# Opening of an attention kernel: layout and order of the first loads, and the order of the first products

## The chip, the cores and the metric

The kernel runs on one core of a Trainium2 chip. The metric is the device time of one execution in microseconds (us): 339.38 is the median of three runs (339.26 to 340.31). The profile is of one further execution, whose own time was 339.0 us; its span from first to last instruction is 337.2 us.

A core has a matmul engine (TensorE, PE in the rows, with its weight loads as PEld), three elementwise engines (VectorE or DVE, ScalarE or ACT, GpSimd or POOL), and a queue of instructions (SyncE, SP) which here issues all transfers between HBM and the on-chip memory SBUF. Matmul results appear in eight banks of another memory, PSUM. Each engine takes its instructions in order; semaphores order the engines against each other.

## What is computed

One layer with causal attention and a linear feed-forward part, both followed by a layer norm, for 1024 tokens of width 512, in float32. Cut to what matters:

```python
q = (x @ Wq) -> 32 heads of 16;  k, v = (x @ Wkv) -> 8 groups of 16 each (4 heads share a group)
scores = q @ k.T, causal; weights = softmax(scores / 4); ctx = weights @ v
x = layernorm(x + ctx @ Wo + bo)
x = layernorm(x + x @ W.T + bias + lora(x))
```

## The kernel before

**Precision by parts.** A float32 operand of a product is split into a high half (the value rounded to a type that TensorE takes at full speed, made by ScalarE) and a low half (the remainder, made by VectorE, later by GpSimd). A product of two operands is three matmuls: high by high, high by low, low by high. So one projection of 128 output columns for 512 tokens, over an inner dimension of 4 chunks of 128, is 12 matmuls of 512 columns. K and Q results are then split into three bf16 parts: ScalarE copies the first (L732), VectorE makes the rest (L958), ScalarE the middle part (L737), VectorE (in the opening, L968) or GpSimd (L582) the low part.

**Units.** Work is done in 16 units, one for each half of the tokens (queries) and each group of 4 heads. For every unit the maxima of the scores are found first, from score matmuls (L1135, called chunks; `chunk_scores` on TensorE, `chunk_max` on VectorE, L917 and L910), then the scores are computed again with the maximum subtracted as additional rows of the operand (L1359), the exponential is taken (ScalarE, L856) and multiplied with V (L1337). The rows come from small bf16 operands QS (queries) and KS (keys) with the parts of a head stacked on the partitions. For all units but the first, the parts are stored to HBM (L479) and loaded back in that arrangement (`load_keys` L490, `load_queries` L502); for the first unit they are moved within the chip by matmuls with selecting matrices: `direct_keys` (3 matmuls) and `direct_queries` (12), L1149, whose results ScalarE (L750, L755) and VectorE (L1070) copy to KS and QS. I call these the move of K and the moves of Q.

**The opening.** `PLAN_A` names the first eight jobs in TensorE's order and how many chunks must have been issued when each ends: K, Q part 0, V, Q part 1, the turning of V, Q part 2, then K and V of the second half of the tokens. Each job is cut in three parts, and chunks stand between parts. The first chunk stands behind the first third of Q part 1; it waits until all four moved queries and the moved keys have been copied. The moves of Q stand behind the second third of V, the move of K between Q part 0 and V.

The transfers are issued in this order by the queue: K's weights wk (L467), the four chunks of the turned x, first half of the tokens (L465, `load_turned(0)`), the part of Wq for Q part 0 (L470), V's weights wv (L471), the rest of Wq (L472), and x's second half (L465). Each is its own semaphore; all are 256 KB but the rest of Wq, 768 KB. A row of x's chunk is a run of 2 KB in HBM; wk, wv and the first part of Wq come in four runs of 512 B for each partition, the rest of Wq in runs of 1.5 KB.

ScalarE's list starts: high half of wk (L818), of x's chunks 0 to 3 (L815), of the first part of Wq (L803), the first part of K's result (L732), high half of wv (L824), middle part of K, high half of Wq's part 1, first part of Q, copy of the moved keys, middle part of Q, high halves of Wq's parts 2 and 3, two copies of moved queries. VectorE's (L1046 and on) starts with the low halves in the same order (L1048, L1043, L1053), then the rest of K (L958), the low half of wv (L962), the low part of K (L968), and the same two for Q. GpSimd makes constants and selecting matrices until 13 us, then the low halves of Wq's parts 1 to 3 (L599) and of x's second half (L606). TensorE begins with nine idle matmuls (`run_idle`, L1288); products are L1195, in `halves`, called by `pe_job`.

K takes its products chunk by chunk of x as the halves come; Q part 0 waits for its weights and has all of its products behind K's.

## Time and profile before

| | |
|---|---|
| median of three runs | 339.38 us (339.26 to 340.31) |
| the profiled execution | 339.0 us, of which the span is 337.2 |
| TensorE busy | 322.3 us, 96% of the span |
| VectorE, ScalarE, GpSimd busy | 256.6, 216.5, 135.3 us |
| mean granted TensorE clock | 0.996 of full speed |
| chain that ended last, by engine | PE 71%, DMA 7%, DVE 7%, ACT 4%, issue 4%, queue 3%, POOL 2% |

Matmuls are pipelined: one of 512 columns lasts 0.4 us or more in the rows while the next starts 0.2 us after it, so starts are to be compared, and the starts of weight loads (PEld) show them best. A row that merges several instructions gives the start of the first, the time from there to the end of the last, and their number. In brackets is how long the engine had been idle and what released it.

### The profile page before, as it was taken

How to read it: one execution, taken by the hardware profiler on the slowest of the kernel's cores; microseconds unless marked ns; L12 is line 12 of the kernel's file. 1: busy time of each engine (PE TensorE's matmuls, PEld its weight loads, DVE VectorE, ACT ScalarE, POOL GpSimd, SP SyncE). 2: the span in 40 equal slices, each digit the busy share in tenths (PEclk: the TensorE clock that was granted, in tenths of full speed). 3: DMA queues.
4: the chain of work that ended last, by engine and by line, in shares of the span. 5: the costliest groups of instructions: out<-in, count | busy, mean ns of one | idle time of the engine just before them, and what ended most of it. 6: DMA issues, size and time to landing. Idle time of an engine off the chain costs nothing.

```text
span 337.2 us, 7240 instructions
## 1 busy us (share of the span) xinstructions
PE 322.3 (96%) x2487; PEld 169.7 (50%) x2487; DVE 256.6 (76%) x787; ACT 216.5 (64%) x418; POOL 135.3 (40%) x268
## 2 busy tenths in 40 slices
PE   8999989999999999999999999999999999999992
PEld 3676445455353344454444544544544434558882
DVE  3557968978888899888889889888886961047664
ACT  4754737645657796848757668478585786952431
POOL 8845325433547585347222123212141122331553
PEclk9999999999999999999999999999999999999998
DMA  6886494874244120020010100000000000000002
GB/s 202 289 163 170 132 183 120 225 230 118 53 148 155 36 63 5 3 47 3 3 48 33 48 4 3 0 31 3 3 0 3 32 2 1 2 33 1 0 33 93
DMA packets 16643, 22.96 MB, mean 68 GB/s; under 512 B 3232, under 2 KB 10560, under 8 KB 16608
## 3 DMA queue, kind: packets, MB, share of 16 engines
q1 hardware_dynamic: 16608, 22.51, 24.4%
q8 instruction: 20, 0.33, 0.4%
q14 instruction: 15, 0.12, 0.1%
HBM read 16.29 MB, written 6.03 MB: 66 GB/s over the span
## 4 chain that ended last, share of the span: by engine, by line
PE 71%; DMA 7%; DVE 7%; ACT 4%; issue 4%; SPq 3%; POOL 2%; POOLq 0%; DVEq 0%; ACTq 0%
PE PS L1337 18%; PE PS L1195 16%; PE PS L1135 15%; PE PS L1359 15%; DMA QS<-NMR 3%; ACT PB L856 2%; PE PS L1263 2%; PE PS L1255 2%; DVE scrap L917 2%; DVE MX L910 2%; DMA scr_q<-parts 2%; DMA X<-in_L_attn_x_turned_dram 1%; SPq L490 1%; PE PS L1149 1%; SPq L502 1%
## 5 line engine op out<-in xcount | busy, mean ns | idle before, releaser
L856 ACT ACTIVATE PB<-PS 128x512 f32<-128x512 f32 x288 | 155.6, 604 | 59.1 <-PE PS L1359 57.9
L917 DVE CUSTOM_DVE_ANT_0 scrap<-PS,mask 128x128 bf16<-128x128 f32 (+3 forms) x256 | 111.5, 487 | 17.6 <-PE PS L1135 17.1
L1135 PE MATMUL PS<-KS,QS 96*128 96x512 bf16 (+3 forms) x384 | 107.9, 329 | 2.1 <-DVE MX L910 1.0
L1359 PE MATMUL PS<-QS,KS 99*128 99x512 bf16 x288 | 106.2, 381 | 1.8 <-DMA QS<-NMR 1.4
L910 DVE TENSOR_REDUCE MX<-PS 128x1 f32<-128x512 f32 x128 | 81.9, 684 | 12.4 <-PE PS L1135 11.7
L696 POOL TENSOR_SCALAR_AFFINE_SELECT PB<-PB 128x256 f32<-128x256 f32 (+1 forms) x96 | 46.4, 485 | 104.3 <-ACT PB L856 101.2
L1337 PE MATMUL PS<-PB,VX 128*32 128x256 f32 (+1 forms) x1280 | 78.8, 364 | 0.6 <-ACT PB L856 0.3
L1135 PEld LDWEIGHTS PS<-KS,QS 96*128 96x128 bf16 x384 | 32.9, 98 | 49.4 <-issue 13.6
L1337 PEld LDWEIGHTS PS<-PB,VX 128*32 128x32 f32 x1280 | 33.5, 109 | 41.9 <-issue 19.0
L1195 PE MATMUL PS<-XT,WQ 128*128 128x512 f32 x144 | 45.4, 439 | 0.5 <-ACT NMR L744 0.4
L1359 PEld LDWEIGHTS PS<-QS,KS 99*128 99x128 bf16 x288 | 27.5, 98 | 31.4 <-ACT PB L856 7.9
L1195 PEld LDWEIGHTS PS<-XT,WQ 128*128 128x128 f32 x144 | 26.6, 193 | 9.5 <-DVE XT L1043 1.5
L1195 PE MATMUL PS<-XT 128*128 128x512 f32 x96 | 28.1, 426 | 0.6 <-DVE MX L910 0.6
L1195 PE MATMUL PS<-WQ,XT 128*128 128x512 f32 x96 | 28.3, 427 | 0.0
L677 POOL TENSOR_SCALAR mv<-mv 128x1 f32<-128x1 f32 x15 | 3.4, 228 | 48.7 <-DVE mv L1012 48.6
L917 DVE DVE_READ_ACCUMULATOR2_ANT MX<- 128x1 f32 x256 | 21.2, 83 | 0.0
L1195 PEld LDWEIGHTS PS<-XT 128*128 128x128 f32 x96 | 17.9, 189 | 4.6 <-DVE MX L910 1.1
L1195 PEld LDWEIGHTS PS<-WQ,XT 128*128 128x128 f32 x96 | 17.9, 189 | 4.1
L770 ACT ACTIVATE RAW<-PS 128x256 f32<-128x256 f32 x32 | 12.4, 387 | 11.2 <-PE PS L1337 11.0
L788 ACT ACTIVATE TC<-RAW,shift,rstd 128x512 f32<-128x512 f32 x7 | 5.7, 817 | 13.4 <-POOL shift L679 13.4
L732 ACT ACTIVATE parts<-PS 128x512 bf16<-128x512 f32 x10 | 6.0, 597 | 10.7 <-PE PS L1195 10.7
L658 POOL CAST NMPS<-NM 128x16 bf16<-128x16 f32 x15 | 3.3, 221 | 21.7 <-DVE NM L931 21.7
(93 smaller groups left out, 263.6 us busy)
## 6 DMA issues: line engine op xcount, KB each, us to landing
scr_q<-parts SPq DMA_DIRECT2D x8, 384.0 KB, 4.0
QS<-scr_q SPq DMA_DIRECT2D x15, 192.0 KB, 2.9
X<-in_L_attn_x_turned_dram SPq DMA_DIRECT2D x8, 256.0 KB, 6.3
X<-in_L_attn_x_dram SPq DMA_DIRECT2D x8, 256.0 KB, 3.1
out_dram<-TC SPq DMA_DIRECT2D x8, 256.0 KB, 2.0
QS<-scr_q SPq DMA_DIRECT2D x15, 128.0 KB, 3.0
RAW<-in_L_attn_Wo_dram SPq DMA_DIRECT2D x2, 512.0 KB, 5.9
RAW<-in_L_ffn_W_dram SPq DMA_DIRECT2D x2, 512.0 KB, 9.0
```

What stands on the lines that cost most here:

```text
L696: nc.gpsimd.affine_select(out=blk, in_=blk, compare_op=ALU.is_ge, fill=0.0, base=0, pattern=[[0, len(heads)], [1, P]], channel_multiplier=-1)\
L732: nc.scalar.activation(parts[:, m % 2, 0, :], job_bank(n), ACT.Copy).then_inc(act_copied, 1)
L770: nc.scalar.activation(RAW[:, u, cols], PS[:, PV_BANK, cols], ACT.Copy).then_inc(raw_out, 1)
L856: nc.scalar.activation(PB[:, cyc % NP_BUF, k, :], PS[:, score_bank(e), :], ACT.Exp, scale=SCALE)\
L910: nc.vector.tensor_reduce(part[:, j0:j1, 0:1], bank, AX, ALU.max).then_inc(max_read, 1)
L917: last = nc.vector.tensor_tensor_reduce(out=scrap[:, n % 2, (j - j0) * width:(j - j0 + 1) * width], in0=bank[:, j - j0, :], in1=mask[:, HT ...
L1135: last = nc.tensor.matmul(PS[:, CHUNK_BANK[n], k * width:(k + 1) * width], QS[0:ROWS, u % SLOTS, j, qb * P:(qb + 1) * P], KS[0:ROWS, g, k0 ...
L1195: last = nc.tensor.matmul(bank, lhs(a, c), rhs(b, c), start=(k == 0), stop=(k == len(terms) - 1))
L1255: last = nc.tensor.transpose(bank[:, g * P:(g + 1) * P], RAW[:, h * G + g0 + g, qb * P:(qb + 1) * P], ident[:, :])
L1263: last = nc.tensor.transpose(bank[:, c * P:(c + 1) * P], src[:, c * P:(c + 1) * P], ident[:, :])
L1337: last = nc.tensor.matmul(PS[32 * j:32 * j + 32, PV_BANK, s * HQ + skip:(s + 1) * HQ], VX[:, key_blocks(cyc)[i], u % G, :], PB[:, cyc % NP ...
L1359: nc.tensor.matmul(PS[:, score_bank(e), :], KS[0:NROW, u % G, kb * P:(kb + 1) * P], QS[0:NROW, u % SLOTS, heads[0]:heads[-1] + 1, s * HQ + ...
```

## The change

1. The host lays Wq and Wkv out so that each partition's piece of a load is one run: wk, wv and Wq's first part 2 KB, the rest of Wq 3 times 2 KB in one piece. Amounts are unchanged.
2. The loads go in the order wk, x's chunks 0 and 1, Wq's first part, x's chunks 2 and 3, wv, the rest of Wq, x's second half. ScalarE and VectorE split in that order, wv too (ahead of K's result).
3. TensorE's first 24 products (`first_products`) go K0, K1, Q0, Q1, K2, Q2, K3, Q3 (the digit is x's chunk), three each. V's twelve follow whole, taking those with the low half of wv last; then the move of K and the moves of Q.
4. ScalarE copies K's and Q's first parts one behind the other, then the middle parts of both, then splits Wq's part 1 and copies the moved keys. VectorE makes both rests, then both low parts.

```diff
@@ -22,9 +22,10 @@
     HD = 16
     H = D // HD
-    G = wkv.shape[2] // HD
+    G = wkv.shape[2] // (D // P) // HD
     REP = H // G
     NC = D // P
     NT = T // P
@@ -337,7 +338,7 @@
         X1B = [TC[:, 4, :], TC[:, 5, :]]
         OUT = [TC[:, 6, :], TC[:, 7, :]]
         a_raw, bT = TC[:, 0, :], TC[:, 8, :]
-        wk_raw, wv_raw = (TC[:, n, :].rearrange("p (c n) -> p c n", c=NC) for n in (2, 3))
+        wk_raw, wv_raw = TC[:, 2, :], TC[:, 3, :]
         bo_bc = TC[:, 4, :]
         vT = TC[:, 5, :]
         rest = TC[:, 6:8, :]
@@ -444,11 +445,14 @@
 
             return x_low[h], c + 1
 
+        def by_chunk(raw):
+            return raw.rearrange("p (c n) -> p c n", c=NC)
+
         def wq_part(half, k):
             return WQ[:, half, :, k * P:(k + 1) * P]
 
         def wq_part_raw(k):
-            return wq_raw[:, :, k * P:(k + 1) * P]
+            return wq_raw[:, k, :].rearrange("p (c n) -> p c n", c=NC)
 
         x_v = x.rearrange("a (h b p) d -> (a h) p b d", h=2, p=P)
         out_v = out.rearrange("a (b p) d -> (a b) p d", p=P)
@@ -458,18 +462,18 @@
 
         @block.sync
         def _(sp):
-            def load_turned(h):
+            def load_turned(h, chunks=range(NC)):
 
                 half = slice(h * HT, (h + 1) * HT)
-                for c in range(NC):
+                for c in chunks:
                     sp.dma_start(XR[:, c, half], xt[c * P:(c + 1) * P, half]).then_inc(x_in[h][c], 16)
 
-            sp.dma_start(wk_raw, wkv[0].rearrange("(c p) n -> p c n", p=P)).then_inc(wk_in, 16)
-            load_turned(0)
-            wq_v = wq.rearrange("(c p) n -> p c n", p=P)
-            sp.dma_start(wq_raw[:, :, 0:P], wq_v[:, :, 0:P]).then_inc(wq_in, 16)
-            sp.dma_start(wv_raw, wkv[1].rearrange("(c p) n -> p c n", p=P)).then_inc(wv_in, 16)
-            sp.dma_start(wq_raw[:, :, P:D], wq_v[:, :, P:D]).then_inc(wq_rest_in, 16)
+            sp.dma_start(wk_raw, wkv[0]).then_inc(wk_in, 16)
+            load_turned(0, range(0, 2))
+            sp.dma_start(wq_raw[:, 0, :], wq[:, 0, :]).then_inc(wq_in, 16)
+            load_turned(0, range(2, NC))
+            sp.dma_start(wv_raw, wkv[1]).then_inc(wv_in, 16)
+            sp.dma_start(wq_raw[:, 1:NC, :], wq[:, 1:NC, :]).then_inc(wq_rest_in, 16)
 
             def parts_to_dram(n):
 
@@ -815,18 +819,20 @@
                 nc.scalar.activation(XT[:, 0, c, half], XR[:, c, half], ACT.Copy).then_inc(x_high, 1)
 
             act.wait_ge(wk_in, 16)
-            nc.scalar.activation(WQ[:, 0, :, D:D + KD], wk_raw, ACT.Copy).then_inc(wk_high, 1)
-            for c in range(NC):
-                x_high_half(0, c)
+            nc.scalar.activation(WQ[:, 0, :, D:D + KD], by_chunk(wk_raw), ACT.Copy).then_inc(wk_high, 1)
+            x_high_half(0, 0)
+            x_high_half(0, 1)
             wq_high_half(0)
+            x_high_half(0, 2)
+            x_high_half(0, 3)
+            act.wait_ge(wv_in, 16)
+            nc.scalar.activation(WQ[:, 0, :, D + KD:D + 2 * KD], by_chunk(wv_raw), ACT.Copy).then_inc(wv_high, 1)
             act_job(JOB["K", 0, 0])
-            act.wait_ge(wv_in, 16)
-            nc.scalar.activation(WQ[:, 0, :, D + KD:D + 2 * KD], wv_raw, ACT.Copy).then_inc(wv_high, 1)
+            act_job(JOB["Q", 0, 0])
             middle_part(0)
+            middle_part(1)
             wq_high_half(1)
-            act_job(JOB["Q", 0, 0])
             direct_keys()
-            middle_part(1)
             wq_high_half(2)
             wq_high_half(3)
             for j in (0, 2):
@@ -957,16 +963,6 @@
                     s = m % 2
                     nc.vector.tensor_tensor(rest[:, s, :], bank, parts[:, s, 0, :], ALU.subtract)\
                         .then_inc(job_freed, 1)
-                    if m == 0:
-                        dve.wait_ge(wv_high, 1)
-                        nc.vector.tensor_tensor(WQ[:, 1, :, D + KD:D + 2 * KD], wv_raw,
-                                                WQ[:, 0, :, D + KD:D + 2 * KD].bitcast(F32), ALU.subtract)\
-                            .then_inc(wv_split, 1)
-                    if m < 2:
-                        dve.wait_ge(rest_split, m + 1)
-                        dve.wait_ge(*freed(JOBS[n]))
-                        nc.vector.tensor_tensor(parts[:, s, 2, :], rest[:, s, :], parts[:, s, 1, :], ALU.subtract)\
-                            .then_inc(parts_ready, 1)
                 else:
                     nc.vector.tensor_tensor(w_raw[:, c, :], bank, w_raw[:, c, :], ALU.add).then_inc(job_freed, 1)
 
@@ -1045,15 +1041,27 @@
 
             nc.vector.memset(Z[:, :], 0.0).then_inc(zeros, 1)
             dve.wait_ge(wk_high, 1)
-            nc.vector.tensor_tensor(WQ[:, 1, :, D:D + KD], wk_raw, WQ[:, 0, :, D:D + KD].bitcast(F32), ALU.subtract)\
+            nc.vector.tensor_tensor(WQ[:, 1, :, D:D + KD], by_chunk(wk_raw), WQ[:, 0, :, D:D + KD].bitcast(F32), ALU.subtract)\
                 .then_inc(wk_split, 1)
-            for c in range(NC):
-                x_low_half(0, c)
+            x_low_half(0, 0)
+            x_low_half(0, 1)
             dve.wait_ge(wq_high, 1)
             nc.vector.tensor_tensor(wq_part(1, 0), wq_part_raw(0), wq_part(0, 0).bitcast(F32), ALU.subtract)\
                 .then_inc(wq_split, 1)
+            x_low_half(0, 2)
+            x_low_half(0, 3)
+            dve.wait_ge(wv_high, 1)
+            nc.vector.tensor_tensor(WQ[:, 1, :, D + KD:D + 2 * KD], by_chunk(wv_raw),
+                                    WQ[:, 0, :, D + KD:D + 2 * KD].bitcast(F32), ALU.subtract).then_inc(wv_split, 1)
+            dve_job(JOB["K", 0, 0])
+            dve_job(JOB["Q", 0, 0])
+            for m in range(2):
+                dve.wait_ge(rest_split, m + 1)
+                dve.wait_ge(*freed(PROJ[m]))
+                nc.vector.tensor_tensor(parts[:, m, 2, :], rest[:, m, :], parts[:, m, 1, :], ALU.subtract)\
+                    .then_inc(parts_ready, 1)
             dve.wait_ge(consts, 3)
-            for n in range(NJOB_A):
+            for n in range(2, NJOB_A):
                 for part in range(3):
                     if part == 2:
                         dve_job(n)
@@ -1195,6 +1203,21 @@
                     last = nc.tensor.matmul(bank, lhs(a, c), rhs(b, c), start=(k == 0), stop=(k == len(terms) - 1))
                 return last
 
+
+            def first_products():
+
+                pe.wait_ge(wk_high, 1)
+                for kind, c in (("K", 0), ("K", 1), ("Q", 0), ("Q", 1), ("K", 2), ("Q", 2), ("K", 3), ("Q", 3)):
+                    n, col, high, low = {"K": (0, D, wk_high, wk_split), "Q": (1, 0, wq_high, wq_split)}[kind]
+                    for k, (a, b) in enumerate(((0, 0), (1, 0), (0, 1))):
+                        pe.wait_ge(*((high, 1), (low, 1), x_split(0, c))[k])
+                        if k == 0:
+                            pe.wait_ge(x_high, c + 1)
+                        last = nc.tensor.matmul(job_bank(n), WQ[:, a, c, col:col + P], XT[:, b, c, 0:HT],
+                                                start=(c == k == 0), stop=(c == NC - 1 and k == 2))
+                    if c == NC - 1:
+                        last.then_inc(job_done, 1)
+
             def pe_job(n, part, parts=3):
 
                 kind, h, c = JOBS[n]
@@ -1208,25 +1231,18 @@
                 if kind in ("K", "V", "Q"):
                     if part == 0:
 
-                        if (kind, h) not in (("K", 0), ("Q", 0)) or c:
+                        if (kind, h) != ("V", 0):
                             pe.wait_ge(*{"K": (wk_split, 1), "V": (wv_split, 1), "Q": (wq_split, c + 1)}[kind])
                         if kind != "K":
                             for cc in range(NC):
                                 pe.wait_ge(*x_split(h, cc))
-
                     terms, ready = TERMS, {}
-                    if (kind, h) == ("K", 0):
-                        terms = [(cc, a, b) for cc in range(NC) for a, b in ((0, 0), (1, 0), (0, 1))]
-                        for cc in range(NC):
-                            ready[cc, 0, 0] = [(x_high, cc + 1)] + ([(wk_high, 1)] if cc == 0 else [])
-                            ready[cc, 1, 0] = [(wk_split, 1)] if cc == 0 else []
-                            ready[cc, 0, 1] = [x_split(0, cc)]
                     if (kind, h) == ("K", 1):
                         for cc in range(NC):
                             ready[cc, 0, 0] = [x_split(1, cc)]
-                    if (kind, h, c) == ("Q", 0, 0):
+                    if (kind, h) == ("V", 0):
                         terms = [(cc, 0, b) for cc in range(NC) for b in (0, 1)] + [(cc, 1, 0) for cc in range(NC)]
-                        ready = {(0, 0, 0): [(wq_high, 1)], (0, 1, 0): [(wq_split, 1)]}
+                        ready = {(0, 0, 0): [(wv_high, 1)], (0, 1, 0): [(wv_split, 1)]}
                     col = {"K": D, "V": D + KD, "Q": c * P}[kind]
                     last = halves(bank, lambda a, cc: WQ[:, a, cc, col:col + P],
                                   lambda a, cc: XT[:, a, cc, half], part, parts, terms, ready)
@@ -1290,17 +1306,17 @@
             pe.wait_ge(zeros, 1)
             run_idle(9)
             pe.wait_ge(consts, 1)
-            for n in range(NJOB_A):
+            first_products()
+            for n in range(2, NJOB_A):
                 for part in range(3):
                     pe_job(n, part)
                     for k in chunks_of_job(n, part):
                         chunk_scores(k)
-                    if JOBS[n] == ("V", 0, 0) and part == 1:
+                    if JOBS[n] == ("V", 0, 0) and part == 2:
+                        direct_keys()
                         direct_queries()
                     if JOBS[n] == ("V", 1, 0) and part == 1:
                         direct_rows()
-                if JOBS[n] == ("Q", 0, 0):
-                    direct_keys()
             pe.wait_ge(consts, 6)
             FIRST_BEHIND = {3 + n % RING: JOBS[n] for n in range(NJOB_A - RING, NJOB_A)}
 
@@ -1421,8 +1437,10 @@
     wkv = wkv.reshape(d, -1, 2, hd)
     laid = dict(inputs)
     laid["L0_attn_x_turned"] = x[0].T
-    laid["L0_attn_Wq"] = wq.reshape(d, nc, 128 // hd, hd).transpose(0, 1, 3, 2).reshape(d, d)
-    laid["L0_attn_Wkv"] = _np.stack([wkv[:, :, 0].transpose(0, 2, 1).reshape(d, -1), wkv[:, :, 1].reshape(d, -1)])
+    wq = wq.reshape(nc, 128, nc, 128 // hd, hd).transpose(1, 2, 0, 4, 3)
+    laid["L0_attn_Wq"] = wq.reshape(128, nc, d)
+    wkv = _np.stack([wkv[:, :, 0].transpose(0, 2, 1).reshape(d, -1), wkv[:, :, 1].reshape(d, -1)])
+    laid["L0_attn_Wkv"] = wkv.reshape(2, nc, 128, -1).transpose(0, 2, 1, 3).reshape(2, 128, -1)
     laid["L0_ffn_lora_B"] = _np.asarray(inputs["L0_ffn_lora_B"]).transpose(0, 2, 1).reshape(128, d)
     laid["L0_ffn_W"] = _np.asarray(inputs["L0_ffn_W"]).T
     laid["L0_ffn_lora_weights"] = _np.repeat(_np.asarray(inputs["L0_ffn_lora_weights"]), 16).reshape(128, 1)
```

## Rows read from the trace of the kernel before

**Rows 1.** Stretches: length, busy us (count) of PE, PEld, DVE, ACT, POOL, clock, DMA

```profile
33.40:50.00 16.60, 14.61 (x103) 7.41 (x103) 14.53 (x65) 9.27 (x17) 4.96 (x11) 1.00 0.76 156
...
100.00:150.00 50.00, 49.31 (x425) 22.27 (x425) 44.83 (x132) 38.10 (x79) 31.15 (x50) 1.00 0.19 52
```

**Rows 2.** Timeline of TensorE: start, us, line, tiles, count [idle <-releaser]

```profile
1.24 4.02 PE L1288 MATMUL PS<-Z 128*128 128x512 bf16 x9 [1.24 <-DVE Z L1046]
...
5.68 0.29 PEld L1195 LDWEIGHTS PS<-XT,WQ 128*128 128x128 f32 x1 [0.25 <-DVE XT L1043]
...
7.02 0.19 PEld L1195 LDWEIGHTS PS<-XT,WQ 128*128 128x128 f32 x1 [0.31 <-DVE XT L1043]
...
9.61 2.82 PEld L1195 LDWEIGHTS PS<-XT,WQ 128*128 128x128 f32 x13 [0.43 <-DVE XT L1043]
...
12.98 0.38 PEld L1149 LDWEIGHTS PS<-parts,PB 128*96 128x96 bf16 x3 [0.55 <-DVE parts L968]
...
13.45 1.79 PEld L1195 LDWEIGHTS PS<-XT,WQ 128*128 128x128 f32 x8
...
15.76 2.32 PEld L1149 LDWEIGHTS PS<-parts,PB 128*96 128x96 bf16 x12 [0.51 <-DVE parts L968]
...
18.17 1.79 PEld L1195 LDWEIGHTS PS<-XT,WQ 128*128 128x128 f32 x8
...
20.24 0.23 PEld L1135 LDWEIGHTS PS<-KS,QS 96*128 96x128 bf16 x4 [0.27 <-issue]
```

**Rows 3.** Timeline of ScalarE: splits and copies of the opening

```profile
3.51 0.63 ACT L818 ACTIVATE WQ<-TC 128x512 fp32r<-128x512 f32 x1 [1.44 <-DMA TC<-in_L_attn_Wkv_dram]
...
4.23 0.63 ACT L815 ACTIVATE XT<-X 128x512 fp32r<-128x512 f32 x1
...
5.61 0.63 ACT L815 ACTIVATE XT<-X 128x512 fp32r<-128x512 f32 x1 [0.75 <-DMA X<-in_L_attn_x_turned_dram]
...
8.20 0.63 ACT L815 ACTIVATE XT<-X 128x512 fp32r<-128x512 f32 x1 [0.60 <-DMA X<-in_L_attn_x_turned_dram]
...
9.01 0.63 ACT L803 ACTIVATE WQ<-RAW 128x512 fp32r<-128x512 f32 x1 [0.18 <-DMA RAW<-in_L_attn_Wq_dram]
...
10.14 0.60 ACT L732 ACTIVATE parts<-PS 128x512 bf16<-128x512 f32 x1 [0.50 <-PE PS L1195]
...
12.89 0.60 ACT L732 ACTIVATE parts<-PS 128x512 bf16<-128x512 f32 x1 [0.16 <-PE PS L1195]
...
14.88 1.14 ACT L803 ACTIVATE WQ<-RAW 128x512 fp32r<-128x512 f32 x2
```

**Rows 4.** Timeline of the queue: the issue of Wq's first part

```profile
3.25 0.43 SPq L470 DMA_DIRECT2D RAW<-in_L_attn_Wq_dram  x1
```

**Rows 5.** Stretches with their DMA share and GB/s at the end

```profile
3.00:7.20 4.20, 4.20 (x12) 1.92 (x10) 2.12 (x3) 2.12 (x4) 3.96 (x13) 1.00 0.87 253
7.50:8.70 1.20, 1.02 (x4) 0.48 (x3) 0.74 (x1) 0.60 (x2) 1.14 (x4) 1.00 1.06 314
...
11.00:13.00 2.00, 1.87 (x10) 1.21 (x8) 1.83 (x3) 1.53 (x4) 1.94 (x2) 1.00 1.05 386
```

**Rows 6.** Timeline of VectorE: last copy of moved queries

```profile
18.59 0.69 DVE L1070 CAST QS<-PS 96x512 bf16<-96x512 f32 x1 [0.61 <-PE PS L1149]
```

**Rows 7.** Timeline of GpSimd: low half of Wq's part 1

```profile
13.21 1.30 POOL L599 TENSOR_TENSOR WQ<-RAW,WQ 128x512 fp32r<-128x512 f32 x1
```

**Rows 8.** Chain of waits, in order of time, and ScalarE's copy of the rows

```profile
26.09 2.56 DMA scr_q<-parts
...
45.21 4.76 DMA QS<-NMR
...
43.29 0.27 ACT L744 ACTIVATE NMR<-PS 48x128 bf16<-48x128 f32 x1
```

**Rows 9.** Timelines: six key loads issued, first chunk of unit 1

```profile
19.60 2.79 SPq L490 DMA_DIRECT2D KS<-scr_k  x6
...
31.36 0.40 PE L1135 MATMUL PS<-KS,QS 96*128 96x128 bf16 x4
```

## The prediction

> **What bounds the kernel now.** I began with the table of stretches. From 50 us on TensorE has no room: in the stretch 100 to 150 it is busy 49.31 of 50 us [rows 1], and nothing there is tied to the clock on the wall, only to the work before it. So whatever the opening is shorter by should arrive at the end, if the stretch from 20 to 50 us passes it on. The change touches the first 20 us alone, so the quantity to forecast is one moment: the first score matmul of the maxima, "chunk 0", which starts at 20.24 [rows 2]. The weight loads on TensorE's queue show what stands before it. The last product of K's first half waits 0.43 us for VectorE and starts at 9.61; it and Q's twelve run 0.22 us apart ((2.82 - 0.19)/12). The move of K waits until 12.98, eight V products follow 0.23 apart, the moves of Q wait 0.51 us until 15.76, take 2.41 us (to 18.17), then four V and four Q products, then chunk 0 [rows 2]. That is 44 matmuls in 10.63 us; at 0.22 they need 9.7, so 0.9 us of it is waiting. Before 9.61 TensorE is starved: 12 products in the time that the loads of x leave it.
>
> The loads show themselves on ScalarE, which splits each as it lands: wk 3.51, x's chunk 0 4.23, chunk 1 5.61, chunk 3 8.20 (1.32 a step on average), wq's part 9.01 [rows 3]. The queue has issued them all much earlier, by 3.68 [rows 4], so the 16 DMA engines set the pace, not the issues.
>
> **What the change removes, adds and moves.** No matmul, copy or byte goes. TensorE has the same 55 matmuls before chunk 0: 24 products of K and Q, 12 of V, 3 + 12 moves, 4 of the next Q. Nine of Q's products (chunks 0 to 2) move ahead of K's last one, into idle time; V's twelve come together, ahead of both moves; and wq's part is loaded third of five, not last.
>
> *When wq's part is split.* It is now behind x's chunk 1, as x's chunk 2 was. Its 256 KB in runs of 2 KB are a load such as trace of before has in this stretch only for x: step 1.32, so ScalarE starts it at 5.61 + 1.32 = 6.93. The bounds: at the 314 GB/s of the stretch in which wq's part and V's weights went in runs of 512 B, 262 KB take 0.83 us, so 6.44; at the 386 GB/s of later 2 KB loads 0.68, so 6.29 [rows 5]. On the slow side, x's first step was 1.38 and the last two 1.30 each on average; one of 1.6, 0.2 beyond the longest, makes 7.2. I take 6.9, because the nearest row has both the size of run and the stretch. The first load, wk, gets the same runs; I leave it where it is, with 0.2 us either way (its 262 KB at 314 and at 386 GB/s differ by 0.15; at 253 it would be 0.2 longer than at 314). x's chunks 2 and 3 go back by one step, to 8.3 and 9.6.
>
> The Trainium skill, "DMA: Bandwidth & Descriptors", Specifications, gives 512 B as the least transfer at full rate; by that the longer runs gain nothing at all. The trace agrees only in part: full-rate stretches show 314 GB/s with mostly 512 B and 386 with 2 KB, yet the cold loads of x, already in 2 KB, reach 253 [rows 5]. By the rule the run length is worth 0, by the two faster rows 0.15 us a load; the sum has 0.
>
> *To K's last product.* From ScalarE's start on a chunk to the weight load that waited for its low half 1.41 us pass (8.20 to 9.61) [rows 2, 3]. TensorE takes its stream in order, so Q's second product starts at 6.9 + 1.41 = 8.3, and all behind it is ready in time or nearly so: thirteen steps of 0.22 later, at 11.17, comes K's last product. (x's chunk 3 alone would allow 9.6 + 1.41 = 11.0.) So K is finished 1.5 us later than now, Q's last product starts at 11.8; it is 12.24 now (9.61 + 2.82 - 0.19).
>
> *To the moves.* K's last product and Q's three: 0.88. V's twelve at 0.22 to 0.23: 2.7. K's three moves: 0.6 (now 0.47 from 12.98 to 13.45, with weight loads running ahead). Q's moves could start at 11.17 + 4.15 = 15.3. Do they find their data? From the start of ScalarE's copy of Q to the moves 12.89 to 15.76, 2.87, go by now, and K's chain took 10.14 to 12.98, 2.84 [rows 2, 3]. Q's copy can start 0.53 after its last weight load, as K's does now (9.61 to 10.14), at 12.3, so the parts are there at 15.2: just in time. VectorE has both rests back to back, then both low parts, and V's low half (one more half such as x's, now between them) falls before K's rest. V's weights are split on ScalarE ahead of K's copy, a wait that is new in this place: K's copy, Q's copy and both middle parts stand behind it. It costs nothing as long as V's weights land by about 10.9; one more load of 1.32 after 9.6 is 10.9. That cover is thin: each 0.1 us beyond it goes on the path.
>
> *To chunk 0.* 2.41 for Q's moves, four products at 0.23 and the 0.27 of the issue wait [rows 2]: 3.6, so 18.9. VectorE's last copy ends 18.59 + 0.69 - 15.76 = 3.52 after the moves' start [rows 6], at 18.8. ScalarE now has the two last splits of wq (1.14 [rows 3]) between its copy of K's move and its two of Q's; from K's last move at 15.1 that is 0.53, 0.6, 1.14 and 1.2 more: 18.5. Both fit, with little to spare. GpSimd's low half of wq's part 1 takes 1.30 [rows 7], from about 15.1, and is used at 17.7. Chunk 0 at 18.9 for 20.24: **1.4 us** earlier.
>
> *Passed on?* From 20 to 50 the path runs through the queue: the store of Q's second part at 26.09, key and query loads, at 45.21 the maxima's move, which lands at 49.97 where TensorE waits for it; the rows for that move are ready on ScalarE at 43.56 [rows 8]. That both arms start from work behind chunk 0 says that both come 1.4 us earlier. What doesn't come 1.4 earlier are the keys of the other units, whose loads follow the landing of Q's first parts: those are ready 0.5 earlier, not 1.4. The six loads are issued from 19.60, over by 22.39, and are wanted at 31.36 [rows 9]; even 5 us to landing (the last move of the maxima took 4.76) leaves 4 us, then 3. So all of 1.4 passes. Against the profiled execution (span 337.2, time 339.0) this is 337.6; against the median 339.38, which lies 0.4 above it, 338.0. I forecast 338.0.
>
> **Rivals.**
> - *The runs pay.* Wq's part is split at 6.3 to 6.5 and wk lands 0.15 sooner; the whole stream behind Q's second product moves with it one to one, to a gain of 1.8 to 2.2: about 337.4. For it: the rates of 314 and 386. Against: 253 in the very stretch.
> - *Loads later than taken.* Five cold 2 KB loads, each as x's, and wk too; the in-order stream waits at Q's first product with K's behind it. Every 0.1 us costs 0.1: at 7.3 the gain is 1.0, at 8.3 none. Likewise V's weights landing after 10.9, held before K's copy. About 338.8.
> - *Absorbed.* Chunk 0 comes as forecast, but one link between 20 and 50 does not: VectorE is busy 14.53 of 16.60 us there [rows 1]. About 339.2. Against: its work also hangs on chunk 0.
> - *Slower: TensorE's clock.* The granted column reads 1.00, yet idle matmuls of 512 columns take 4.02 us for nine, 0.43 apart with the tail of the last, the 1.2 GHz level, and 0.22 is that of 2.4; K's weight loads fall from 0.29 to 0.19 us between 5.68 and 7.02 [rows 2], so that is where the level rises. In the changed kernel TensorE has one product between 7.2 and 8.3 us, while it waits for wq. If it stays or falls back to 1.2 GHz there, a product costs 0.21 more: seven of them eat the gain, twelve make it slower by more than 0.3%, and the 18 products from there to V's make 3.8 - 1.4 = 2.4 slower, 341.8. Against it: waits of 0.25 and 0.31 us between products now did not keep the level from rising, and one of 0.43 did not bring it down.
>
> The Trainium skill, "TensorE: Matmul & The Clock Gate", Part 1, says that the array's default is the half rate, that activity releases it and idleness brings it back. The rise in the trace agrees; no row of before shows a fall in the opening.
>
> **How the numbers follow.** Forecast 0.48 (gain 1.05 to 1.8: 337.6 to 338.3); runs pay 0.15; loads later 0.15; absorbed 0.15; clock 0.07. What a measurement here can tell from no change is about 0.3%, 1.0 us. Faster: 0.48 + 0.15 = 0.63. Within: 0.15 + 0.15 = 0.30. Slower 0.07. The range goes from 337.0 (a gain of 2.4) to 339.5 (nothing left, and the scatter of the runs), which leaves out the slower case and little else.
>
> **What would show it.** In the changed kernel's rows: ScalarE's split of wq near 6.9 and x's last near 9.6; one unbroken run of products from 8.3 with K's last at 11.2 and Q's 0.66 behind; no idle before K's move; Q's moves from 15.3; chunk 0 at 18.9; the maxima's move landing at 48.6. If wq is split at 6.4 or before, the step of 1.32 was wrong; if weight loads take 0.29 after 8.3, the clock rival holds; if chunk 0 is early and 49.97 hasn't moved, it is absorbed. A gap before Q's moves says that the chain of parts, with V's split before it, was late.

## The result: slower by 0.7%, and the profile after

The changed kernel takes 341.63 us (median of 22 executions, 339.26 to 344.27), the kernel before 339.83 in the same runs (338.34 to 340.43). The ratio is 1.0067, with a 95% interval of 1.0048 to 1.0085: slower by 1.6 to 2.9 us, where 1.4 us faster had been forecast. The profiled execution took 340.97 us with a span of 339.3, 2.1 us more than that of before. Comparisons here leave out executions that are more than 1.5% above the fastest of their kernel.

ScalarE's timeline of the changed kernel shows what came when; it answers to [rows 3]. L819 are x's chunks, L807 Wq's parts, L829 V's weights, L736 the first parts of K and Q.

```profile
3.51 0.63 ACT L822 ACTIVATE WQ<-TC 128x512 fp32r<-128x512 f32 x1 [1.44 <-DMA TC<-in_L_attn_Wkv_dram]
4.12 0.63 ACT L819 ACTIVATE XT<-X 128x512 fp32r<-128x512 f32 x1
5.41 0.63 ACT L819 ACTIVATE XT<-X 128x512 fp32r<-128x512 f32 x1 [0.65 <-DMA X<-in_L_attn_x_turned_dram]
8.32 0.63 ACT L807 ACTIVATE WQ<-RAW 128x512 fp32r<-128x512 f32 x1 [2.28 <-DMA RAW<-in_L_attn_Wq_dram]
9.77 1.28 ACT L819 ACTIVATE XT<-X 128x512 fp32r<-128x512 f32 x2 [0.82 <-DMA X<-in_L_attn_x_turned_dram]
11.08 0.63 ACT L829 ACTIVATE WQ<-TC 128x512 fp32r<-128x512 f32 x1
14.84 1.29 ACT L736 ACTIVATE parts<-PS 128x512 bf16<-128x512 f32 x2 [3.13 <-PE PS L1216]
```

K's weights and x's chunks 0 and 1 are there as forecast or sooner. Wq's first part is 2.9 us behind chunk 1, not 1.3: the engine stood idle for 2.28 us. The loads issued behind it are late too. ScalarE waits 0.82 us more for x's chunk 2 and starts it at 9.77, where 8.3 was forecast, so here it could have split nothing in the meantime. From the issue of Wq's load to its landing:

```profile
DMA to landing us min/median/max: 6.1/6.1/6.1
```

TensorE's weight loads, which answer to [rows 2] (the last row is chunk 0):

```profile
6.98 0.19 PEld L1216 LDWEIGHTS PS<-XT,WQ 128*128 128x128 f32 x1 [0.53 <-DVE XT L1039]
9.00 0.19 PEld L1216 LDWEIGHTS PS<-XT,WQ 128*128 128x128 f32 x1 [1.83 <-ACT WQ L807]
9.73 5.34 PEld L1216 LDWEIGHTS PS<-XT,WQ 128*128 128x128 f32 x17 [0.54 <-DVE WQ L1049]
15.11 2.69 PEld L1203 LDWEIGHTS PS<-XT,WQ 128*128 128x128 f32 x12
17.84 3.15 PEld L1157 LDWEIGHTS PS<-parts,PB 128*96 128x96 bf16 x15
...
22.30 0.24 PEld L1143 LDWEIGHTS PS<-KS,QS 96*128 96x128 bf16 x4 [0.35 <-issue]
```

Between the last product of chunk 1 (6.98) and Q's second product (9.73) there is one product. Then 17 products take 5.34 us, 0.32 each, where [rows 2] has 0.22. The moves start without a wait (17.84). The stretches say why the products are slow; the columns are the stretch, its length, busy us (count) of TensorE, the granted clock as a share of 2.4 GHz, and the DMA engines' busy share and GB/s:

```profile
5.00:7.00 2.00, 1.76 (x6) 1.00 0.91 207
7.00:9.00 2.00, 0.48 (x1) 1.00 0.89 284
9.00:11.00 2.00, 1.78 (x7) 1.00 1.02 410
11.00:13.00 2.00, 2.00 (x6) 0.51 0.98 384
13.00:15.00 2.00, 2.00 (x7) 0.64 0.34 131
15.00:17.00 2.00, 2.00 (x11) 1.00 0.00 1
```

In 7 to 9 us TensorE is busy 0.48 of 2 us; from 11 on the granted clock is at its lower level (1.2 GHz) for about 3.4 us ((1 - 0.51) x 2 / 0.5 and (1 - 0.64) x 2 / 0.5), then back at 2.4. Chunk 0 starts at 22.30 and not 20.24. The chain of waits leads from Wq's load to the first transfer of the maxima's rows:

```profile
2.17 6.13 DMA RAW<-in_L_attn_Wq_dram
...
9.73 5.77 PE PS L1216 x17
...
47.48 4.79 DMA QS<-NMR
```

It lands at 52.27; from [rows 8] it was 49.97. So 2.1 us at chunk 0 became 2.3 at 52 us and 2.1 at the end.

Three explanations were to be told apart: **A**, TensorE's clock falls because it idles; **B**, runs of 2 KB are slow this early; **C**, the load's place in the order. Later B was split into **D/F**, the distance between the runs, **G**, the spread over untouched memory, and **E**, the run length as such.

### The profile page after: what moved, and what is told of

Its sections match the earlier page's. It is cut to its first block, busy times and chain, and to the rows that moved or that the text cites. A ratio compares the mean times of both kernels' runs of the same rounds, so it can differ in the third digit from the quotient of the medians.

```text
span 339.3 us, 7246 instructions
## 1 busy us (share of the span) xinstructions
PE 322.7 (95%) x2487; PEld 170.9 (50%) x2487; DVE 256.6 (76%) x787; ACT 216.3 (64%) x418; POOL 134.4 (40%) x268
## 4 chain that ended last, share of the span: by engine, by line
PE 72%; DMA 8%; DVE 6%; issue 4%; ACT 4%; SPq 3%; POOL 2%; POOLq 0%; DVEq 0%; ACTq 0%
PE PS L1353 18%; PE PS L1203 16%; PE PS L1143 15%; PE PS L1375 15%; DMA QS<-NMR 3%; ACT PB L862 2%; PE PS L1279 2%; PE PS L1271 2%; DMA scr_q<-parts 2%; DVE scrap L923 2%; DVE MX L916 2%; DMA RAW<-in_L_attn_Wq_dram 2%; PE PS L1216 2%; SPq L494 1%; SPq L506 1%
## 5 line engine op out<-in xcount | busy, mean ns | idle before, releaser
L1203 PE MATMUL PS<-XT,WQ 128*128 128x512 f32 x120 | 37.5, 435 | 0.4 <-ACT NMR L748 0.4
L1203 PEld LDWEIGHTS PS<-XT,WQ 128*128 128x128 f32 x120 | 22.0, 190 | 5.9 <-ACT NMR L748 1.3
L736 ACT ACTIVATE parts<-PS 128x512 bf16<-128x512 f32 x10 | 6.0, 597 | 13.4 <-PE PS L1203 10.2
```

Source lines behind the costliest of these rows:

```text
L1203: last = nc.tensor.matmul(bank, lhs(a, c), rhs(b, c), start=(k == 0), stop=(k == len(terms) - 1))
```

## Experiments

Each kernel is compared with the kernel before on the same chip. The experiments ran on four chips (e1 to e4, e5 to e8, e9 to e12, e13 to e15), so kernels of different groups are compared only through the kernel before. The ratio is not the quotient of the two medians beside it. Where the two differ much (e7, e10, e11, e13), the size of the effect is the less certain.

"Landing" is issue to landing of Wq's first part in the one profiled execution. It is comparable between the kernels of this table, which load that part third (behind x's chunk 1). One trace each is thin: the same loads landed in 4.6 and 5.5 us (e2 and e4), and, two places later in the order, in 5.5 and 6.4 (e11 and e15).

| kernel | runs of Wq's first part | landing, us | median, before's | ratio, 95% |
|---|---|---|---|---|
| changed | 2 KB, 8 KB apart | 6.1 | 341.63, 339.83 | 1.0067 (1.0048 to 1.0085) |
| e13 changed, again | the same | 6.4 | 341.28, 339.95 | 1.001 (0.9968 to 1.0051) |
| e3 idle matmuls | the same | 6.7 | 341.51, 340.14 | 1.0025 (0.9999 to 1.0051) |
| e10 | 2 KB, 16 KB apart | 4.3 | 341.56, 339.67 | 1.0023 (0.999 to 1.0056) |
| e9 | 2 KB, 10 KB apart | 4.4 | 339.06, 339.67 | 0.9976 (0.9951 to 1.0002) |
| e5 | 2 KB, one piece | 4.3 | 338.34, 339.97 | 0.9956 (0.9928 to 0.9984) |
| e14 | 2 KB, one piece | 4.8 | 338.36, 339.95 | 0.9945 (0.9917 to 0.9974) |
| e6, x too | 2 KB, one piece | 4.8 | 338.96, 339.97 | 0.9971 (0.9947 to 0.9994) |
| e2 | 512 B, 2 KB apart | 4.6 | 339.18, 340.14 | 0.9967 (0.9939 to 0.9994) |
| e4, e2 with idle matmuls | 512 B, 2 KB apart | 5.5 | 341.03, 340.14 | 1.002 (0.9995 to 1.0045) |
| e7 | 512 B, 2 KB apart | 4.3 | 338.87, 339.97 | 0.9989 (0.996 to 1.0018) |

### The layout or the order: e1 and e2

e1 is the kernel before with change 1 alone; e2 is the changed kernel without it. Of e2's edit against the changed kernel, the line that loads Wq's first part:

```diff
-            sp.dma_start(wq_raw[:, 0, :], wq[:, 0, :]).then_inc(wq_in, 16)
+            sp.dma_start(wq_raw[:, :, 0:P], wq_v[:, :, 0:P]).then_inc(wq_in, 16)
```

> The kernel before with the new layout alone: wk, wv and Wq's first part in runs of 2 KB, order of loads and of products as before. Theory A (the clock fall made the change slow, the runs are neutral): within 0.5 us of before, Wq's part split near 9.0. Theory B (2 KB runs from HBM are slow to land this early): Wq's part is split at 9.8 or later and x's chunks shift too, 0.7 to 1.5 us slower than before. Theory C (the place of Wq's load in the order made it late): as A, no difference.

> The changed kernel with the old layout: runs of 512 B, but the new order of loads and products. Theory A: the clock still falls when TensorE waits for Wq, so still 1 to 2 us slower than before. Theory B: Wq's part is split at 6.5 to 6.9 and not at 8.3, the stream runs from 8.0, TensorE hardly waits, the clock stays, and the kernel is 1 to 2 us faster than before. Theory C: Wq's part still at 8 or later, as slow as the changed kernel.

e1: 0.9985 (0.996 to 1.001), no difference. But its ScalarE timeline shows the slow load even there, 2.05 us behind x's chunk 3, where [rows 3] has 0.81:

```profile
7.81 0.63 ACT L817 ACTIVATE XT<-X 128x512 fp32r<-128x512 f32 x1 [0.45 <-DMA X<-in_L_attn_x_turned_dram]
9.86 0.63 ACT L805 ACTIVATE WQ<-RAW 128x512 fp32r<-128x512 f32 x1 [1.41 <-DMA RAW<-in_L_attn_Wq_dram]
```

K's chain doesn't wait for it, and the executions show no loss, though in this trace chunk 0 came at 20.89, 0.65 us later than before. e2: 0.9967 (0.9939 to 0.9994), 1.1 us faster. The new layout costs nothing measurable in the old order, the new order gains with the old layout, and only both together lose: C falls. TensorE's weight loads of e2 are the forecast nearly to the letter, Q's second product at 8.37 (8.3), chunk 0 at 19.32 (18.9), the clock at 1.00:

```profile
8.37 3.73 PEld L1217 LDWEIGHTS PS<-XT,WQ 128*128 128x128 f32 x17 [0.40 <-DVE WQ L1050]
...
14.86 3.15 PEld L1158 LDWEIGHTS PS<-parts,PB 128*96 128x96 bf16 x15
...
19.32 0.24 PEld L1144 LDWEIGHTS PS<-KS,QS 96*128 96x128 bf16 x4 [0.35 <-issue]
```

### The clock: e3, e4, e15

All three have ten idle matmuls where TensorE waits for Wq: e3 is the changed kernel with them, e4 is e2 with them, e15 is described below.

```diff
+                        if (kind, c) == ("Q", 0) and k < 2:
+                            run_idle((8, 2)[k])
```

> The changed kernel with ten more idle matmuls: eight before the first product of Q, two before its second, where TensorE waits for Wq's part. Nothing else differs. Theory A: the granted clock stays at 1.00, eight products at 0.43 become 0.22, so about 1.7 us faster than the changed kernel, close to before (0 to +0.5 us). Theory B or C alone (the late load is all of the loss): no change against the changed kernel, +2 us against before.

> Old layout, new order, with the ten idle matmuls. If the runs of 2 KB make the load late (B) and the clock is the other half (A), this is the fastest of the four, 1 to 1.5 us faster than before, a little behind the kernel without idle matmuls where the clock stays anyway. If the place in the order makes the load late (C), it is like the kernel with idle matmuls and the new layout, level with before.

e3 gets 1.0025 where the changed kernel had 1.0067; the changed kernel's second measurement (e13, 1.001) can't be told from it, so the executions alone don't show that filling helps here. The trace does: the load is as late (6.7), and the 17 products take 3.75 us, at a granted clock of 1.00, for 5.34, and chunk 0 comes at 21.30 for 22.30:

```profile
9.00:11.00 2.00, 1.39 (x6) 1.00 1.03 418
11.00:13.00 2.00, 2.00 (x11) 1.00 1.02 398
```

```profile
9.61 0.19 PEld L1218 LDWEIGHTS PS<-XT,WQ 128*128 128x128 f32 x1 [1.17 <-ACT WQ L807]
...
10.33 3.75 PEld L1218 LDWEIGHTS PS<-XT,WQ 128*128 128x128 f32 x17 [0.27 <-DVE WQ L1049]
```

e4 missed what I expected of an early load: 1.002 (0.9995 to 1.0045), slower than e2. The idle matmuls are themselves in the way. In its trace (of an execution of 344.79 us, 3.8 above its median, with x's chunk 1 late as well) the last product of x's chunk 1 starts at 8.52, the idle ones run until 10.3, and the high half of Wq had been ready since 8.5. Filling is a trade, not a gift.

### Lateness by order alone: e11 and e15

e11 has the fast layout (e5's), but issues Wq's part behind x's chunks 2 and 3, while the engines still take it third. e15 adds the ten idle matmuls to that. Of e11's edit, against e5:

```diff
-            load_turned(0, range(0, 2))
+            load_turned(0)
             sp.dma_start(wq_raw[:, 0, :], wq[0]).then_inc(wq_in, 16)
-            load_turned(0, range(2, NC))
```

> Wq in one piece per part (the fast layout), but its first part issued behind x's chunks 2 and 3, while ScalarE, VectorE and TensorE still take it in third place. It makes Wq late by order alone: split at 7.8 to 8.5, as late as in the changed kernel. If lateness in that place is the whole mechanism (TensorE stands with Q's first product, and the clock may fall), it gives back most of the gain of the early one: 1 to 2 us slower than the same layout with Wq third, +0 to +1 us against before. If the layout costs in another way than by this wait, it stays 1 us or more faster than before.

> The kernel with Wq in one piece but issued too late (behind x's chunks 2 and 3, +1.8 us against before), with eight idle matmuls ahead of Q's first product and two ahead of its second, so that the wait is as long but TensorE isn't idle in it. If the fall of TensorE's clock is a cost of its own beside the wait, the eight or so products at half rate (0.43 for 0.22 each) go: granted clock 1.00 from 5 to 20 us, 1 to 1.7 us faster than without them, +0.1 to +0.8 us against before. If the wait is all, no change: +1.8 us.

e11: 1.0053 (1.0026 to 1.0079), 1.8 us slower than before, 3.3 slower than the same layout in time (e5, through before), and beyond the 0 to 1 us that I expected. The split is at 8.60, x's chunks 2 and 3 had landed and stood behind it in ScalarE's list, and the clock falls as in the changed kernel:

```profile
5.66 0.63 ACT L818 ACTIVATE XT<-X 128x512 fp32r<-128x512 f32 x1 [0.75 <-DMA X<-in_L_attn_x_turned_dram]
8.60 0.63 ACT L806 ACTIVATE WQ<-RAW 128x512 fp32r<-128x512 f32 x1 [2.31 <-DMA RAW<-in_L_attn_Wq_dram]
```

```profile
7.00:9.00 2.00, 0.64 (x2) 1.00 1.04 395
9.00:11.00 2.00, 1.71 (x3) 0.55 1.06 408
11.00:13.00 2.00, 2.00 (x7) 0.60 0.92 339
13.00:15.00 2.00, 2.00 (x11) 1.00 0.04 14
```

e15: 0.9985 (0.9956 to 1.0014), no difference from before. The loss is gone, but so is the gain: a late load with TensorE kept busy about cancels the forecast 1.4. From e15 to e11 it is 2.3 us by the ratios, whose intervals do not meet, and that is what the idle matmuls save: 3.4 us at half the clock are 1.7 of it. I had expected 1 to 1.7. e15's one trace shows the clock at 1.00 from 5 to 23 us but not the time: it is of an execution of 343.58 us, 3.3 above its median, in which x's chunk 0 was split at 5.70 and Wq's part at 9.51, and chunk 0 of the maxima came at 22.88.

```profile
22.88 0.24 PEld L1142 LDWEIGHTS PS<-KS,QS 96*128 96x128 bf16 x4 [0.35 <-issue]
```

### What makes the load late: e5, e6, e7, e9, e10, e14

e5 stores Wq part by part, so that each part is one piece of 256 KB; e6 does the same with x's chunks; e7 puts only Wq back to 512 B; e9 and e10 pad Wq's rows to 10 and 16 KB; e14 takes the first part out into one piece, and leaves the rest in runs of 6 KB, as the changed kernel has them, but now directly behind one another. Of e5's edit:

```diff
-            sp.dma_start(wq_raw[:, 0, :], wq[:, 0, :]).then_inc(wq_in, 16)
+            sp.dma_start(wq_raw[:, 0, :], wq[0]).then_inc(wq_in, 16)
...
-    wq = wq.reshape(nc, 128, nc, 128 // hd, hd).transpose(1, 2, 0, 4, 3)
-    laid["L0_attn_Wq"] = wq.reshape(128, nc, d)
+    wq = wq.reshape(nc, 128, nc, 128 // hd, hd).transpose(2, 1, 0, 4, 3)
+    laid["L0_attn_Wq"] = wq.reshape(nc, 128, d)
```

> The changed kernel with Wq laid out part by part: runs of 2 KB as in the changed kernel, but those of the first part lie directly behind one another (256 KB in one piece), not 8 KB apart. Theory D (it is the distance of the runs, 8 KB, that makes Wq's load slow): Wq's part is split one step of 0.8 to 1.3 us behind x's chunk 1, near 6.5, the clock stays, 2.5 to 3.5 us faster than the changed kernel, so 0.5 to 1.2 faster than before. Theory E (2 KB runs of Wq are slow wherever they lie): as the changed kernel, Wq's split at 8 or later and +2 us against before.

> As the one with Wq in one piece, and x's eight chunks too, each 256 KB in one piece (now runs of 2 KB, 4 KB apart). Theory D: x's steps fall from 1.3 to 0.8 or so as well, last split of x near 7.5 to 8, 1 to 2 us faster than before. Theory E: x's steps stay at 1.3, no gain over the one with Wq alone.

> The changed kernel with Wq alone back in runs of 512 B (2 KB apart); wk and V's weights keep 2 KB. If Wq's load is all that the layout does, this equals the kernel with the old layout and the new order (about 1 us faster than before, Wq's split near 6.5 to 6.9). If wk's runs matter too, it lies between that and the changed kernel.

> The changed kernel with Wq's rows padded, so that the 2 KB runs of its first part lie 10 KB apart and not 8 KB; same bytes loaded. Theory F (the distance hurts because it is a power of two, so that the runs of one load meet in the same places of HBM): issue to landing of Wq's part falls from 6.1 to 6.7 us to 4.3 to 4.8 us, as with one piece; about 1.5 us faster than before. Theory G (it hurts because the load is spread over 1 MB of HBM that nothing has read yet): 6.1 us or more again, as slow as the changed kernel, +1.5 to +2.5 us against before.

> The same with the runs 16 KB apart, a larger power of two and a wider spread (2 MB). Theory F: landing later than with 8 KB, 7 us or more after the issue, +3 us or more against before. Theory G: also later than with 8 KB, so it tells only together with the 10 KB run: F wants 10 KB fast and 16 KB slow, G wants both slow. If both are as with 8 KB, the distance as such has reached its full price at 8 KB.

> The changed kernel with only Wq's first part taken out into one piece of 256 KB (runs of 2 KB directly behind one another); the rest of Wq stays in runs of 6 KB, as in the changed kernel. In the run with all of Wq part by part both had changed. If the distance of 8 KB of the first part is the cause, this one is as fast as that: 0.3 to 0.5% faster than before. If the 6 KB runs of the rest, queued behind it, are, it is as slow as the changed kernel.

> The changed kernel itself, beside the two others on one chip, so that they are compared with it directly, and for a second trace of it. If the first result holds, about 0.6% (2 us) slower than before; issue to landing of Wq's part over 6 us in its trace if that is its usual value, nearer 4.5 if it is a matter of luck in each execution.

e5: 0.9956, 1.5 us faster than before, against a forecast of 1.4 for the change. The load of 2 KB runs in one piece is ready when x's chunk 1 has been split (6.49 is the end of that split, not a landing):

```profile
5.85 0.63 ACT L819 ACTIVATE XT<-X 128x512 fp32r<-128x512 f32 x1 [1.11 <-DMA X<-in_L_attn_x_turned_dram]
6.49 0.63 ACT L807 ACTIVATE WQ<-RAW 128x512 fp32r<-128x512 f32 x1
7.16 0.63 ACT L819 ACTIVATE XT<-X 128x512 fp32r<-128x512 f32 x1
7.97 0.63 ACT L819 ACTIVATE XT<-X 128x512 fp32r<-128x512 f32 x1 [0.19 <-DMA X<-in_L_attn_x_turned_dram]
```

```profile
DMA to landing us min/median/max: 4.3/4.3/4.3
```

So runs of 2 KB as such are not slow: E falls. e14 is as fast, 0.9945 (0.9917 to 0.9974), with all twelve executions between 336.57 and 339.56, so runs of 6 KB in the rest do no harm either. **Wq's rows 8 KB apart are the cause of the late load, and the late load of the loss.** Third in the order, such a load landed after 6.1, 6.4 and 6.7 us, and every other one of the table after 4.3 to 5.5. Whether it is the spacing of the first part alone is not separated: e5, e9 and e14 change that of the rest as well, which is queued behind it. e6 with x in one piece too gains nothing further (0.9971): x's spacing of 4 KB costs nothing that shows, though its interval covers e5's. e7 (0.9989, interval up to 1.0018) lies between and is not told from no change, with a trace as good as e5's up to chunk 0 (18.87); what it lost in its profiled execution is told below.

Why 8 KB hurts is not settled. 10 KB is 0.8 us faster than before (upper end of the interval 1.0002) with a landing of 4.4, although it spreads wider than 8 KB, which speaks against G. 16 KB should have been worse than 8 KB under F, 3 us or more over before with a landing of 7. Its median is 1.9 us over before, its interval reaches from 0.999 to 1.0056, and its one trace shows a landing of 4.3, in an execution that was among its three fastest (338.87 of 338.31 to 345.64; the other nine are at 340.52 or above). It may be that the landing is late in some executions and not in others; no trace of one of the nine exists. x's runs, 4 KB apart, show no cost. So that powers of two are the reason is a guess, which 10 against 8 KB supports and 16 KB leaves open.

The changed kernel, a second time (e13), has a landing of 6.4 and a median of 341.28 for 339.95, but its twelve executions scatter from 339.03 to 346.98, and its ratio of 1.001 (0.9968 to 1.0051) shows no difference from before where I expected 0.6%. On the same chip e14, with twelve executions below 339.6, is clearly faster than it. In e13's trace the clock is low for twice as long, and the 17 products take 6.35 us:

```profile
7.00:9.00 2.00, 0.49 (x1) 0.95 0.96 304
9.00:11.00 2.00, 1.77 (x4) 0.50 1.00 406
11.00:13.00 2.00, 2.00 (x6) 0.50 0.97 376
13.00:15.00 2.00, 2.00 (x6) 0.50 0.27 102
15.00:17.00 2.00, 2.00 (x9) 0.85 0.00 0
```

### The last part alone, and a version that beats both: e8 and e12

e8 is the kernel before with V's products whole and both moves behind them, and Q's middle part ahead of ScalarE's copy of the moved keys; e12 is e5 with Wq's part loaded and split behind x's chunk 0 and products in the order K0, Q0, K1, Q1, K2, Q2, K3, Q3. Of e12's edit, the order of the products:

```diff
-                for kind, c in (("K", 0), ("K", 1), ("Q", 0), ("Q", 1), ("K", 2), ("Q", 2), ("K", 3), ("Q", 3)):
+                for kind, c in (("K", 0), ("Q", 0), ("K", 1), ("Q", 1), ("K", 2), ("Q", 2), ("K", 3), ("Q", 3)):
```

> The kernel before, loads, layout and order of K's and Q's products untouched; only V's twelve products whole, then the move of K, then those of Q, and ScalarE makes Q's middle part ahead of the copy of the moved keys. By my working the two waits of TensorE (0.5 us each) ahead of the moves go, and half as many products stand behind the moves: chunk 0 at 19.3 to 19.5, 0.7 to 0.9 us faster than before. The rival, that the waits come back at the copies of the moved queries, gives 0 to 0.3.

> A version meant to beat both: Wq in one piece per part, loaded behind x's chunk 0 (second place among x's chunks), and products in the order K0, Q0, K1, Q1, K2, Q2, K3, Q3. Wq split near 5.3, TensorE fed in even portions, last product bound by x's chunk 3 (split near 8): chunk 0 at 18.3 to 18.8, 0.3 to 1 us faster than with Wq third, so 1.8 to 2.5 us faster than before. If the parts' chain behind Q (2.9 us) or the copies bind instead, it is level with Wq third, 1.5 us faster than before.

e8: 0.9978 (0.9958 to 0.9999), 0.7 us faster, the lower end of what I had worked out; 25 products in one row, then fifteen moves, then chunk 0 at 19.60:

```profile
9.56 5.54 PEld L1195 LDWEIGHTS PS<-XT,WQ 128*128 128x128 f32 x25 [0.43 <-DVE XT L1043]
15.14 3.15 PEld L1149 LDWEIGHTS PS<-parts,PB 128*96 128x96 bf16 x15
...
19.60 0.24 PEld L1135 LDWEIGHTS PS<-KS,QS 96*128 96x128 bf16 x4 [0.35 <-issue]
```

e12: 0.9941 (0.9906 to 0.9976), 338.18 for 339.67, 2.0 us faster than before, and beside e14's the lowest ratio. Its trace doesn't show the gain over e5 that I expected: Wq landed 4.8 after its issue, was split at 6.49 only, and chunk 0 came at 19.56. The interval covers e5's and e14's, so nothing says that it is better than those. All three beat the kernel before, and their intervals lie wholly below that of the first result.

## Why the prediction was wrong

- **What bounds the kernel, and that the opening passes on: right for a loss.** 2.1 us at chunk 0, 2.3 at the maxima's landing, 2.1 at the end. For a gain the medians agree (1.6 us less in e5 and e14), but the traces do not show its way. In the eight kernels of the new order whose load was in time and not behind idle matmuls (e2, e5, e6, e7, e9, e10, e12, e14) chunk 0 comes 0.7 to 1.4 us earlier than before; the maxima's rows that are wanted near 72 us come between 0.7 us earlier (e5) and 1.3 later (e7), and only e5 (336.4) and e10 (337.1) have a span below the 337.2 of before, whose profiled execution (339.0) was itself quicker than its medians of 339.38 to 340.14.
- **When Wq's part is split: wrong, the first step that failed.** I took 6.9 with a slow bound of 7.2; it was 8.32. I priced the load by its size and run length, from x's chunks. Their runs lie 4 KB apart, Wq's 8 KB, and no row of before had such a load; e5 and e14 have 6.5 and 7.0 with the same size and run length. x's chunk 2 behind it was late with it (9.77 for 8.3). The bound had to be wider than the scatter of x's steps, since the access was one that the trace doesn't contain. Cost: 9.73 for 8.3, 1.43 us.
- **The in-order stream behind Q's second product: right.** It starts 1.41 us after ScalarE's split (8.32 to 9.73), and everything behind moved one to one.
- **The products at 0.22: wrong, the second step.** 17 took 5.34 for the 3.73 of e2 and e5, 1.6 us more, by the lower clock. I had this as the rival that ends slower, with one product between 7.2 and 8.3. I argued against it from waits of at most 0.43 us, but the wait was 1.8 and 0.5, since the first error made it longer. The two terms aren't independent: a late load both delays the stream and slows it. Its chance of 0.07 should have been that of the load being late, and the case should have carried both prices: 1.4 + 1.6 against a gain of 1.4. That the rival's 341.8 lies near the measured 341.63 is luck: it has 3.8 us of slow products and a load in time.
- **Moves and copies: right in size.** From the start of the moves to chunk 0 4.46 us (17.84 to 22.30) for 0.6 + 3.6; no wait before the moves; V's weights were split at 11.08, just beyond my limit of 10.9, and it didn't matter, because K's copy came at 14.84.
- **The sum.** Forecast 18.9 + 1.43 + 1.6 + 0.3 = 22.2, measured 22.30. With the load in time the forecast gain of 1.4 us is met or nearly so by e2 (1.1), e5 (1.5), e14 (1.9) and e6 (1.0); e9 (0.8) and e7 (0.4) fall short, and neither's interval excludes no gain.
- **The rule on 512 B** (the Trainium skill, "DMA: Bandwidth & Descriptors", Specifications), that full rate is reached there: e7 and e5 show landings of 4.3 us with 512 B and 2 KB alike, one trace each, so no worth of the run length shows here. The same page ("Latency and other measured facts") tells of transfers that slow down with large powers of two between rows; the distances that it measured begin at 512 KB, so it doesn't cover 8 KB, and the runs here leave open whether the like holds there.
- **The clock** (the Trainium skill, "TensorE: Matmul & The Clock Gate", Part 1), that idleness brings the half rate back: the trace agrees, 1.00 until 11 us and then 0.51, behind a stretch in which TensorE was busy 0.48 of 2 us.

## What to carry to other kernels

A transfer is costed by its size, its run length and the distance of its runs; where the trace has no load of the same kind, its landing is unknown, and an engine that takes its work in order should not have it at its head (in e11 x's chunks stood ready behind it). Laying a piece out as one block in HBM was the safe choice. In the traces here no wait of TensorE up to 1.7 us is followed by a lower clock, and each of 2.2 us or more is (e3, e4, e6, e7). Between, both happen: 1.8 to 2.1 us brought it down in the openings of the changed kernel, e11 and e13, where a second wait of about 0.5 us follows one product later, and near 75 us in e9 and e15; it stayed up behind such waits in e2, e8, e10 and e14. So a wait that can grow to about 2 us is priced twice, once as a wait and once as the products behind it at half the clock. And a term that triggers another needs one joint case in the forecast, not two small ones.

## What the runs showed that I had not expected

The clock falls at a second place, mostly in kernels whose opening is good. Between 72 and 78 us TensorE waits for the maxima's rows, a small transfer that lands late while the DMA engines are busy (share 0.99 at 70 to 72 us in e6). In e6 that wait is 2.5 us, and the products behind it run at the lower level:

```profile
72.00:74.00 2.00, 0.43 (x9) 1.00 0.78 221
74.00:76.00 2.00, 1.57 (x6) 0.84 0.06 22
76.00:78.00 2.00, 2.00 (x20) 0.50 0.00 0
78.00:80.00 2.00, 2.00 (x12) 0.81 0.02 4
```

```profile
PEld PS L1375 <- DMA QS<-NMR: 2.5, 1, 2.5
```

e9 and e15 (2.0 us each), e3 (2.2), e4 and e7 (3.2 each) show the same there. The changed kernel (0.9), before (1.1), e5 (1.3), e1 and e12 (1.7 each), e2 and e8 (1.9 each), e14 and e10 (2.1 each) wait and keep the clock. In e10:

```profile
73.63 0.10 PEld L1375 LDWEIGHTS PS<-QS,KS 99*128 99x128 bf16 x1 [2.08 <-DMA QS<-NMR]
```

```profile
74.00:76.00 2.00, 2.00 (x24) 1.00 0.15 45
```

So an execution can lose 1.7 us (3.4 us at half rate) by an event far behind the edited code. Whether it hangs on the opening is open: the kernels with an early chunk 0 wait 1.3 to 3.2 us here, before 1.1, the changed kernel and e11 0.9, but e3 and e15, with a late one, 2.2 and 2.0. The fall of the clock accounts for much of e6's profiled span of 339.4, although its chunk 0 came at 19.38. That it is also what makes single executions scatter by 2 to 5 us is likely, but only the profiled ones show it. The mean granted clock over the executions points the same way: 0.9953 to 0.9957 for before on each of the four chips, 0.9920 for the changed kernel, 0.9919 for e11, and 0.9951 and 0.9968 for e15 and e14.
